# Attention scores of a four-layer kernel on one Trainium2 core: half-height score matmuls, two banks to a tile, and another order of a group's work

## The chip, the core and the metric

The program runs on one of the eight cores of a Trainium2 chip. A core has a matrix engine (TensorE, PE in the profile; its weight loads are listed as PEld), a vector engine (VectorE, DVE), an activation engine (ScalarE, ACT), a general engine (GpSimd, POOL) and a queue that starts transfers (SyncE, SP). Each engine works through its own list of instructions in order and waits on semaphores that the others count up. TensorE writes into PSUM, eight banks of 512 float32 values for each of the 128 partitions; VectorE and ScalarE read them from there. The metric is the device time of the whole program in microseconds (us); lower is better.

## What is computed

Four layers, each an attention followed or accompanied by a gated feed-forward network, on 4 sequences of 256 tokens, 512 wide. The attention has 32 heads of 16 dimensions. In three layers (0, 2 and 3) four query heads share a key head, queries and keys are rotated, and a causal mask applies; layer 1 has its own keys for each head and neither rotation nor mask. Of each attention this is what matters here:

```python
scores = jnp.einsum('bhsd,bhtd->bhst', q, k) / jnp.sqrt(jnp.float32(HEAD_DIM))
scores = jnp.where(causal[None, None], scores, jnp.finfo(scores.dtype).min)   # layers 0, 2, 3
attn = jax.nn.softmax(scores, axis=-1)
out = jnp.einsum('bhst,bhtd->bhsd', attn, v)
```

The four feed-forward networks differ (octonion ternary weights, int4 weights, fp8 scales, low rank); the change does not touch them apart from the names of PSUM banks.

## The kernel before

**Units and groups.** An attention is cut into 8 units `u` (a sequence and one half of the heads: 16 heads), and a unit into 4 groups `g` of 4 heads; `gi = 4u + g` counts the 32 groups of a layer. A unit's queries and keys are first laid out as stacks: a head's 16 dimensions as a rounded value, a low part and the rounded value again, 48 rows, one more row for the maximum, padded to 64. Two heads fill 128 rows. `stack_high` (ACT) and `stack_low` (POOL) write the stacks, `turn_stacks` (PE, L665) turns them with transposes, `take_stacks` (ACT, L1026) and `take_key_stacks` (DVE, L1378) copy them out of PSUM as `qT` and `kT`. Before the change a key's stack stands twice, once above 64 rows of zeros and once below them, so that a matmul of all 128 rows gives the scores of one head alone.

**Scores, twice.** `scores_rows` (L685) makes the scores with queries as partitions, with a second matmul (L691, an identity against a bf16 mask) that adds the mask; `row_max` (DVE, L1370) takes the negated maximum. The maxima of a unit are turned (`turn_max`, L701), copied and placed by a transfer as one row of `qT`. `scores_cols` (L719) then makes the scores with keys as partitions, the maximum already subtracted; `exponentials` (ACT, L1038) writes `probs`; in the causal layers `cut_future` (POOL, L1572) zeroes what lies ahead. `weigh_values` (L739) multiplies the probabilities of the group before by the values, in four column tiles of 32; `take_pv` (ACT, L1045) copies the result, `turn_context` (L750) turns it two groups later, and `context` (DVE, L1394 and L1397) divides by the sum. For every two units the rows are turned (`turn_rows`, L760) and projected (`project_out`, L780); the inputs of later units are projected by `project` (L647). `scores_rows` runs five groups ahead (`LEAD`) of `scores_cols`.

**What sets the order.** The order is written out by hand, for each engine apart, in the function `attention` of that engine: a loop over the 32 groups. Nothing reorders it. In group `g` TensorE has: `project` in g = 0 and 3, `turn_max` in g = 3, first half of `scores_cols`, stacks of tau 0 (g = 0 and 2), first half of `scores_rows`, `weigh_values` of the group before, second half of `scores_cols`, stacks of tau 1, second half of `scores_rows`, `turn_context`, and in every second unit `turn_rows` (g = 2) and `project_out` (g = 3). (In g = 1 the first half of `scores_rows` stands behind `weigh_values`.)

**Banks.** A tile of PSUM is claimed by a key; `Banks` counts the uses of each bank and TensorE waits until the bank's earlier holder has been emptied. A tile of scores is one bank: two heads. `scores_rows` takes turns in banks 0 and 1, `scores_cols` in 2 and 3, everything else in 4 to 7:

```python
def misc_bank():
    misc[0] += 1
    return 4 + misc[0] % 4
```

## Time and profile before

| | us |
|---|---|
| median of 3 runs | 1435.74 (1433.23 to 1436.2) |
| profiled execution, span from first to last instruction | 1432.5 |
| TensorE matmuls busy | 1328.4 (93%) |
| TensorE weight loads busy | 998.8 (70%) |
| VectorE busy | 884.6 (62%) |
| ScalarE busy | 670.5 (47%) |
| GpSimd busy | 389.4 (27%) |

The profile is of one execution, and every duration below is of that one. Its span of 1432.5 us is 3.2 us under the median of the runs; the profile gives no other time of it. A matmul's length includes the time in which it runs through the array while the next has begun, so the distance from start to start is what one costs in a row of many. Where the timeline merges instructions, x is their count and the length runs from the first start to the last end.

### The profile page before, as it was taken

How to read it: one execution, taken by the hardware profiler on the slowest of the kernel's cores; microseconds unless marked ns; L12 is line 12 of the kernel's file. 1: busy time of each engine (PE TensorE's matmuls, PEld its weight loads, DVE VectorE, ACT ScalarE, POOL GpSimd, SP SyncE). 2: the span in 40 equal slices, each digit the busy share in tenths (PEclk: the TensorE clock that was granted, in tenths of full speed). 3: DMA queues.
4: the chain of work that ended last, by engine and by line, in shares of the span. 5: the costliest groups of instructions: out<-in, count | busy, mean ns of one | idle time of the engine just before them, and what ended most of it. 6: DMA issues, size and time to landing. Idle time of an engine off the chain costs nothing.

```text
span 1432.5 us, 22066 instructions
## 1 busy us (share of the span) xinstructions
PE 1328.4 (93%) x8364; PEld 998.8 (70%) x8364; DVE 884.6 (62%) x1661; ACT 670.5 (47%) x1420; POOL 389.4 (27%) x470
## 2 busy tenths in 40 slices
PE   4999899997798999998899999989999879899997
PEld 3888777775465666665688888877777557677775
DVE  7733577777506655567455566467777645777873
ACT  3433365655133654556223333236565447365653
POOL 1000333323011100000433443323343346333331
PEclk9999999999799999999899999999999889999998
DMA  6000000002000000002222232100000300000001
GB/s 261 1 1 0 1 3 2 2 2 97 30 0 1 2 1 2 2 2 92 95 89 88 92 107 89 45 1 2 2 3 2 128 30 1 1 2 2 3 1 60
DMA packets 11610, 48.18 MB, mean 34 GB/s; under 512 B 2793, under 2 KB 3694, under 8 KB 10226
## 3 DMA queue, kind: packets, MB, share of 16 engines
q1 hardware_dynamic: 11506, 46.76, 9.3%
q8 instruction: 69, 1.13, 0.3%
q14 instruction: 35, 0.29, 0.1%
HBM read 44.13 MB, written 2.10 MB: 32 GB/s over the span
## 4 chain that ended last, share of the span: by engine, by line
PE 84%; DVE 10%; ACT 3%; issue 2%; DMA 1%; POOL 0%; SPq 0%; DVEq 0%; ACTq 0%
PE bank L487 18%; PE bank L647 13%; PE bank L518 9%; PE bank L719 7%; PE bank L780 7%; PE bank L685 7%; PE bank L739 7%; PE bank L665 6%; PE bank L691 3%; DVE negmaxs L1370 2%; PE bank L750 2%; DVE negmaxw L1370 2%; PE bank L588 1%; DVE stats L1127 1%; PE bank L760 1%
## 5 line engine op out<-in xcount | busy, mean ns | idle before, releaser
L1572 POOL TENSOR_SCALAR_AFFINE_SELECT probss<-probss 128x512 f32<-128x512 f32 x192 | 134.2, 700 | 334.0 <-ACT probss L1038 334.0
L1370 DVE TENSOR_REDUCE negmaxs<-bank 128x2 f32<-128x512 f32 (+1 forms) x384 | 193.7, 551 | 36.8 <-PE bank L691 35.0
L1038 ACT ACTIVATE probss<-bank 128x256 f32<-128x256 f32 (+1 forms) x384 | 167.9, 492 | 41.9 <-PE bank L719 41.4
L685 PE MATMUL bank<-kTs,qTs 128*128 128x512 f32 (+1 forms) x384 | 135.3, 411 | 5.2 <-DVE kTs L1378 2.8
L1518 POOL TENSOR_TENSOR W_lo<-W_lo_whole,W_hi 128x1536 fp32r<-128x1536 f32 x28 | 98.1, 3504 | 138.4 <-ACT W_hi L889 138.4
L719 PE MATMUL bank<-qTs,kTs 128*128 128x256 f32 (+1 forms) x384 | 117.3, 383 | 4.6 <-ACT probss L1038 3.9
L691 PE MATMUL bank<-mask,identb 128*128 128x256 bf16 x384 | 105.0, 283 | 0.0
L889 ACT ACTIVATE W_hi<-W_lo_whole 128x1536 fp32r<-128x1536 f32 x28 | 41.7, 1488 | 134.7 <-DVE W_lo_whole L1253 134.7
L1378 DVE CAST kTs<-bank 128x512 fp32r<-128x512 f32 x96 | 65.6, 689 | 50.9 <-PE bank L665 50.9
L1274 DVE TENSOR_TENSOR h_lo<-h_lo_whole,h_hi 128x512 fp32r<-128x512 f32 x50 | 73.3, 1465 | 34.9 <-ACT h_hi L911 34.9
L1378 DVE CAST kTw<-bank 128x512 fp32r<-128x512 f32 x64 | 40.9, 685 | 82.3 <-PE bank L665 82.3
L1370 DVE TENSOR_REDUCE negmaxw<-bank 128x2 f32<-128x512 f32 x128 | 81.6, 685 | 14.0 <-PE bank L685 13.6
L487 PE MATMUL bank<-xT_hi,W_hi 128*128 128x512 f32 x224 | 89.2, 398 | 0.0
L487 PE MATMUL bank<-xT_lo,W_hi 128*128 128x512 f32 x224 | 88.6, 396 | 0.0
L685 PEld LDWEIGHTS bank<-kTs,qTs 128*128 128x128 f32 x384 | 74.5, 194 | 20.0 <-DVE negmaxs L1370 11.5
L487 PE MATMUL bank<-xT_hi,W_lo 128*128 128x512 f32 x224 | 88.4, 395 | 0.0
L647 PE MATMUL bank<-Wqkv,xT_whole 128*128 128x512 f32 (+1 forms) x256 | 87.0, 495 | 0.8 <-ACT gate L922 0.8
L987 ACT ACTIVATE qks<-bank 128x320 f32<-128x320 f32 x48 | 21.1, 439 | 141.7 <-PE bank L647 141.6
L739 PE MATMUL bank<-probss,Vs 128*32 128x256 f32 (+1 forms) x1536 | 82.7, 333 | 4.0 <-issue 3.5
L911 ACT ACTIVATE h_hi<-h_lo_whole 128x512 fp32r<-128x512 f32 x72 | 45.4, 630 | 72.3 <-DVE h_lo_whole L1265 46.4
L1038 ACT ACTIVATE probsw<-bank 128x512 f32<-128x512 f32 x128 | 69.6, 599 | 16.6 <-PE bank L719 14.2
L719 PEld LDWEIGHTS bank<-qTs,kTs 128*128 128x128 f32 x384 | 60.4, 191 | 23.4 <-issue 12.7
(219 smaller groups left out, 3162.2 us busy)
## 6 DMA issues: line engine op xcount, KB each, us to landing
W_lo_whole<-in_w SPq DMA_DIRECT2D x28, 768.0 KB, 4.2
Wqkv_whole<-in_Wqkv SPq DMA_DIRECT2D x3, 1536.0 KB, 10.6
Wo_lo_whole<-in_Wo SPq DMA_DIRECT2D x4, 1024.0 KB, 6.2
Wqkv<-in_Wqkv SPq DMA_DIRECT2D x1, 3072.0 KB, 10.6
Wdown_whole<-in_Wd SPq DMA_DIRECT2D x1, 2816.0 KB, 15.2
x<-in_x SPq DMA_DIRECT2D x4, 512.0 KB, 5.9
out<-x SPq DMA_DIRECT2D x8, 256.0 KB, 2.2
V_lo_whole<-in_V SPq DMA_DIRECT2D x1, 1408.0 KB
```

Source lines behind the costliest of these rows:

```text
L487: ins = mm(ps[:], lh, rh, start=(c == 0), stop=(c == len(terms) - 1))
L518: ins = mm(B.tensor(key)[:], lh, rh, start=(j == 0 and c == 0), stop=(j == C - 1 and c == len(terms) - 1))
L647: ins = mm(ps[:, 0:width], lh, rh, start=(c == 0), stop=(c == len(terms) - 1))
L685: ins = mm(ps[:, 0:2 * nk].rearrange("p (h k) -> p h k", h=2), A[l].qT[u % 2][:, 2 * g + pl, qb * P:(qb + 1) * P], A[l].kT[u % 2][:, slot: ...
L691: ins = mm(dst, identb[:], mask[:].rearrange("p (h k) -> p h k", h=2), start=False, stop=True)
L719: ins = mm(ps[:, pairs[0] * nq:pairs[1] * nq].rearrange("p (h q) -> p h q", h=n), A[l].kT[u % 2][:, key_slot(l, g, 2 * g + pairs[0], par), ...
L739: ins = mm(ps[32 * i:32 * i + 32, q0:SEQ], A[l].Vflat[u % 4][:, (kb * A[l].vh + kv) * CELL:(kb * A[l].vh + kv) * CELL + 32], A[l].probs[gi ...
L780: ins = mm(ps[:], lh, rh, start=(c == 0), stop=(c == len(terms) - 1))
L1038: nc.scalar.activation(A[l].probs[gi % 2][:, kb, par:4:2, q0:SEQ], B.tensor(key)[:, 0:2 * nq].rearrange("p (h q) -> p h q", h=2), ACT.Exp, ...
L1370: v.tensor_reduce(A[l].negmax[u % 2][:, qb, 2 * g + pl:2 * g + pl + 9:8], B.tensor(key)[:, 0:2 * nk].rearrange("p (h k) -> p h k", h=2), A ...
L1378: v.tensor_copy(A[l].kT[u % 2][:, 4 * w:4 * w + 4, tau * P:(tau + 1) * P], B.tensor(key)[:].rearrange("p (a t) -> p a t", a=4)).then_inc(B ...
L1572: gp.affine_select(out=blk, in_=blk, compare_op=ALU.is_ge, fill=0.0, base=0, pattern=[[0, 4], [1, P]], channel_multiplier=-1).then_inc(cau ...
```

## The change

**Matmuls of 64 rows.** The zero rows in the key stacks go. A head of a pair is multiplied in the upper 64 rows of the array (`par` 0) and the other in the lower 64 (`par` 1), each into a bank of its own; the mask is added in the same way by four bf16 matmuls of 64 rows with 128 columns (`cut_rows`, `cut_keys`). `kT` has half the slots, and fewer key transposes fill it. Weights are permuted on the host for this.

**Tiles of two banks.** A tile of scores now is all four heads of a group: two adjacent banks, one `row_max` and one `exponentials` instruction in place of two.

**Order and banks.** The loop of TensorE is written anew; ScalarE's and VectorE's loops follow it. Core of the diff:

```diff
-    def claim(self, key, bank):
-        self.where[key] = (bank, self.uses[bank])
+    def claim(self, key, bank, n=1):
+
+        earlier = [self.emptied(k) for k in dict.fromkeys(self.holder[bank:bank + n]) if k is not None]
+        self.where[key] = (bank, self.uses[bank], n)
         self.uses[bank] += 1
+        self.holder[bank:bank + n] = [key] * n
+        return self.tensor(key), earlier
...
-            def misc_bank():
-                misc[0] += 1
-                return 4 + misc[0] % 4
+            def next_bank(n=1):
+
+                if n == 2:
+                    ring[0] += ring[0] % 2
+                bank = ring[0] % 8
+                ring[0] += n
+                return bank
...
+                key = ("S", l, u, g, qb)
+                ps = claim(key, bank, 2)
                 for pl in range(2):
+                    for par in range(2):
+                        r = slice(64 * par, 64 * par + 64)
+                        ins = mm(ps[:, par, pl * nk:(pl + 1) * nk], A[l].qT[u % 2][r, 2 * g + pl, qb * P:(qb + 1) * P],
+                                 A[l].kT[u % 2][r, key_slot(l, g, pl), 0:nk], start=(pl == 0),
+                                 stop=(pl == 1 and not CAUSAL[l]))
+                if CAUSAL[l]:
+                    for j in range(2):
+                        for par in range(2):
+                            r = slice(64 * par, 64 * par + 64)
+                            k0 = nk - P + 64 * j
+                            dst = ps[:, par, 0:2 * nk].rearrange("p (h k) -> p h k", h=2)[:, :, k0:k0 + 64]
+                            ins = mm(dst, cut_rows[r, j, :], cut_keys[r, j, :, :], start=False, stop=(j == 1))
+                ins.then_inc(B.fills(key), 1)
...
                 for gi in range(GROUPS * UNITS):
                     u, g = divmod(gi, GROUPS)
 
                     ahead = gi + LEAD < GROUPS * UNITS
+                    if g == 0 and u + 1 < UNITS:
+                        turn_stacks(l, u + 1, 1)
+                    if g == 2 and u + 2 < UNITS:
+                        turn_stacks(l, u + 2, 0)
                     if g == 0 and u + 2 < UNITS:
                         project(l, u + 2, 1)
+                    if g == 3 and u + 1 < UNITS:
+                        turn_max(l, u + 1)
                     if g == 3 and u + 3 < UNITS:
                         project(l, u + 3, 0)
-                    if g == 3 and u + 1 < UNITS:
-                        turn_max(l, u + 1)
-                    scores_cols(l, u, g, 0)
-                    if g == 0 and u + 1 < UNITS:
-
-                        turn_stacks(l, u + 1, 0, 1)
-                    if g == 2 and u + 2 < UNITS:
-
-                        turn_stacks(l, u + 2, 0, 0)
-                    if ahead and g != 1:
-                        scores_rows(l, gi + LEAD, 0)
-                    if gi >= 1:
-                        weigh_values(l, gi - 1)
-                    if ahead and g == 1:
-
-                        scores_rows(l, gi + LEAD, 0)
-                    scores_cols(l, u, g, 1)
...
+
+                    for part in range(2):
+                        if ahead:
+                            scores_rows(l, gi + LEAD, part, 4 * part)
+                        scores_cols(l, u, g, part, 4 * part + 2)
+                        ring[0] = 4 - 4 * part
+                        if part == 0 and gi >= 1:
+                            weigh_values(l, gi - 1)
                     if gi >= 2:
                         turn_context(l, gi - 2)
...
+                key = ("S", l, u, g, qb)
+                dve.wait_ge(*B.filled(key))
+                v.tensor_reduce(A[l].negmax[u % 2][:, qb, :].rearrange("p (b h) -> p b h", b=2)[:, :, 2 * g:2 * g + 2],
+                                B.tensor(key)[:, :, 0:2 * nk].rearrange("p b (h k) -> p b h k", h=2),
+                                AX.X, ALU.max, negate=True).then_inc(B.empties(key), 1)
```

`turn_stacks` now takes both tau in one go and `take_stacks` and `take_key_stacks` follow it. ScalarE's loop has, for each group: `take_stacks`, `take_projection`, first half of `exponentials`, `take_pv`, second half of `exponentials`, `stack_high`, `take_rows`. Here `ring[0]` is what sets the banks: after the first part it is 4, so `weigh_values` takes bank 4; after the second it is 0, so `turn_context` takes bank 0, and what follows it takes 1, 2, 3 and so on.

**TensorE's list, a plain group** (g = 1 of the second unit, first causal layer), from the values matmuls on. A name such as `bank4_emptied` is the semaphore that counts the copies out of that bank (of a two-bank tile, out of its first bank); the numbers in a tile's name tell buffers apart. Before:

```order
L739 MATMUL bank<-probss_103,Vs_82 32x256 [waits bank2_emptied,bank3_emptied,causal_cut,bank6_emptied]
L739 MATMUL bank<-probss_103,Vs_82 32x256 x3
L739 MATMUL bank<-probss_103,Vs_82 32x128 x4
L685 MATMUL bank<-kTs_98,qTs_97 128x256 [waits bank4_emptied,bank7_emptied,bank1_emptied,bank5_emptied]
L691 MATMUL bank<-mask,identb 128x256
L685 MATMUL bank<-kTs_98,qTs_97 128x256 [waits bank0_emptied]
L691 MATMUL bank<-mask,identb 128x256
L719 MATMUL bank<-qTs_99,kTs_100 128x256 [waits bank3_emptied]
L719 MATMUL bank<-qTs_99,kTs_100 128x256 [waits bank2_emptied]
L685 MATMUL bank<-kTs_98,qTs_97 128x512 [waits bank1_emptied]
L691 MATMUL bank<-mask,identb 128x2x128
L685 MATMUL bank<-kTs_98,qTs_97 128x512 [waits bank0_emptied]
```

Of the change, from the last two matmuls of the first half on:

```order
L718 MATMUL bank<-qTs_99,kTs_100 128x512 [waits bank2_emptied]
L718 MATMUL bank<-qTs_99,kTs_100 128x512
L737 MATMUL bank<-probss_103,Vs_82 32x256 [waits bank2_emptied,bank3_emptied,causal_cut,bank4_emptied]
L737 MATMUL bank<-probss_103,Vs_82 32x256 x3
L737 MATMUL bank<-probss_103,Vs_82 32x128 x4
L686 MATMUL bank<-kTs_98,qTs_97 128x256 [waits bank4_emptied]
L686 MATMUL bank<-kTs_98,qTs_97 128x256 x3
L695 MATMUL bank<-cut_keys,cut_rows 128x2x64 x4
L718 MATMUL bank<-qTs_99,kTs_100 128x256 [waits bank6_emptied]
L718 MATMUL bank<-qTs_99,kTs_100 128x256
L747 MATMUL bank<-ident,pvs_106 128x128 [waits bank4_emptied,bank0_emptied]
L747 MATMUL bank<-ident,pvs_106 128x128
```

The first half of `scores_rows` has moved ahead of this place; the second half stands directly behind the values matmuls and waits for bank 4, the bank which these have just filled.

**TensorE's list at g = 2**, where the stacks of a later unit are turned. Before:

```order
L719 MATMUL bank<-qTs_99,kTs_100 128x512 [waits bank3_emptied]
L719 MATMUL bank<-qTs_99,kTs_100 128x512 [waits bank2_emptied]
L665 MATMUL bank<-ident_r,qstacks_87 128x128 [waits stack_lo,bank4_emptied,stack_hi,pads_set]
L665 MATMUL bank<-ident_r,qstacks_87 128x128 x3
L665 MATMUL bank<-ident_r,kstacks_89 128x128 [waits bank5_emptied]
L665 MATMUL bank<-ident_r,kstacks_89 128x128 x3
L685 MATMUL bank<-kTs_98,qTs_97 128x256 [waits bank1_emptied]
L691 MATMUL bank<-mask,identb 128x256
L685 MATMUL bank<-kTs_98,qTs_97 128x256 [waits bank0_emptied]
L691 MATMUL bank<-mask,identb 128x256
L739 MATMUL bank<-probss_104,Vs_82 32x256 [waits bank2_emptied,bank3_emptied,causal_cut,bank6_emptied]
```

Of the change:

```order
L655 MATMUL bank<-ident_r,qstacks_87 128x128 [waits stack_lo,bank0_emptied,stack_hi,pads_set]
L655 MATMUL bank<-ident_r,qstacks_87 128x128 x3
L655 MATMUL bank<-ident_r,qstacks_88 128x128 [waits stack_lo,bank2_emptied,stack_hi,pads_set]
L655 MATMUL bank<-ident_r,qstacks_88 128x128 x3
L667 MATMUL bank<-ident_r,kstacks_89 128x128 [waits bank2_emptied]
L667 MATMUL bank<-ident_r,kstacks_90 128x128
L686 MATMUL bank<-kTs_98,qTs_97 128x128 [waits bank1_emptied,bank0_emptied]
L686 MATMUL bank<-kTs_98,qTs_97 128x128 x3
L695 MATMUL bank<-cut_keys,cut_rows 128x2x64 x4
L718 MATMUL bank<-qTs_99,kTs_100 128x512 [waits bank3_emptied,bank2_emptied]
L718 MATMUL bank<-qTs_99,kTs_100 128x512
```

Both tau of the stacks stand ahead of the group's scores now, with the waits for `stack_hi` and `stack_lo` of both; before, the second tau stood behind the first half.

**VectorE's list of the same plain group.** Before:

```order
L1370 TENSOR_REDUCE negmaxs_111<-bank 128x2 [waits bank1_filled]
L1370 TENSOR_REDUCE negmaxs_111<-bank 128x2 [waits bank0_filled]
L1370 TENSOR_REDUCE negmaxs_111<-bank 128x2 [waits bank1_filled]
L1370 TENSOR_REDUCE negmaxs_111<-bank 128x2 [waits bank0_filled]
L1394 RECIPROCAL recips_116<-bank 128x8 [waits bank6_emptied,bank7_filled]
L1397 TENSOR_TENSOR ctxs_107<-bank,recips_116 128x2x64 [waits reciprocal_ready]
```

Of the change:

```order
L1343 TENSOR_REDUCE negmaxs_111<-bank 128x2x2 [waits bank0_filled]
L1343 TENSOR_REDUCE negmaxs_111<-bank 128x2x2 [waits bank4_filled]
L1371 RECIPROCAL recips_116<-bank 128x8 [waits bank0_emptied,bank0_filled]
L1374 TENSOR_TENSOR ctxs_107<-bank,recips_116 128x2x64 [waits reciprocal_ready]
L1353 CAST kTs_100<-bank 128x256 [waits bank3_filled]
```

Two reductions take the place of four; the division (L1371, L1374) reads bank 0, as the first of the reductions does, and stands behind the second.

## Rows read from the trace of the kernel before

**Rows 1.** The page, part 1: busy us of each engine, share of the span, instructions.

```profile
PE 1328.4 (93%) x8364; PEld 998.8 (70%) x8364; DVE 884.6 (62%) x1661; ACT 670.5 (47%) x1420; POOL 389.4 (27%) x470
```

**Rows 2.** Busy time by stretch, two stretches: length, engines with counts, PEclk (granted clock), DMA.

```profile
165.28:172.10 6.82, 4.30 (x21) 4.30 (x22) 4.41 (x9) 2.43 (x7) 1.41 (x3) 0.50 0.00 1
...
210.00:259.00 49.00, 48.92 (x415) 37.90 (x414) 37.52 (x86) 29.83 (x78) 17.86 (x28) 1.00 0.01 2
```

**Rows 3.** Timeline of PE, first causal layer, values matmuls: start us, length us, engine, line.

```profile
211.32 0.86 PE L739 MATMUL bank<-probss,Vs 128*32 128x256 f32 x16
...
231.29 0.86 PE L739 MATMUL bank<-probss,Vs 128*32 128x256 f32 x16
...
235.91 0.86 PE L739 MATMUL bank<-probss,Vs 128*32 128x256 f32 x16
...
242.92 0.86 PE L739 MATMUL bank<-probss,Vs 128*32 128x256 f32 x16
...
254.43 0.86 PE L739 MATMUL bank<-probss,Vs 128*32 128x256 f32 x16
...
257.76 0.86 PE L739 MATMUL bank<-probss,Vs 128*32 128x256 f32 x16
```

**Rows 4.** Timeline of all engines in one group (u=2, g=3).

```profile
241.79 0.71 PE L719 MATMUL bank<-qTs,kTs 128*128 128x512 f32 x2
...
242.36 1.08 ACT L1038 ACTIVATE probss<-bank 128x512 f32<-128x512 f32 x2
...
243.45 0.48 DVE L1354 TENSOR_TENSOR rope_coss<-qks,cos 128x320 f32<-128x320 f32 x1
...
243.84 0.38 ACT L1045 ACTIVATE pvs<-bank 128x256 f32<-128x256 f32 x1 [0.40 <-PE bank L739]
...
245.29 1.28 DVE L1370 TENSOR_REDUCE negmaxs<-bank 128x2 f32<-128x512 f32 x2
...
246.72 0.29 DVE L1397 TENSOR_TENSOR ctxs<-bank,recips 128x128 f32<-128x128 f32 x1
```

**Rows 5.** Timeline, the first of a group's score tiles and its first maximum.

```profile
183.19 0.19 PEld L685 LDWEIGHTS bank<-kTs,qTs 128*128 128x128 f32 x1 [0.46 <-DVE negmaxs L1370]
...
183.86 1.29 DVE L1370 TENSOR_REDUCE negmaxs<-bank 128x2 f32<-128x512 f32 x2 [0.39 <-PE bank L691]
```

**Rows 6.** Timeline, copies that build the stacks, and one that takes them from PSUM.

```profile
233.60 0.64 ACT L1015 ACTIVATE qstacks<-rope_coss 128x512 fp32r<-128x512 f32 x1
...
234.71 0.74 POOL L1556 TENSOR_TENSOR qstacks<-rope_coss,qstacks 128x256 fp32r<-128x256 f32 x1 [0.30 <-ACT kstacks L1021]
...
235.62 0.60 ACT L1026 ACTIVATE qTs<-bank 128x512 fp32r<-128x512 f32 x1
```

**Rows 7.** Timeline of PE: projections, four key transposes, two score tiles of 256 columns.

```profile
244.90 0.47 PE L780 MATMUL bank<-Wo_hi,ctxTs 128*128 128x512 f32 x1
...
250.59 0.34 PE L647 MATMUL bank<-Wqkv_hi,xT_hi 128*128 128x384 f32 x1
...
252.70 0.62 PE L719 MATMUL bank<-qTs,kTs 128*128 128x512 f32 x2
...
253.45 0.50 PE L665 MATMUL bank<-ident_r,kstacks 128*128 128x128 f32 x4
...
253.79 0.35 PE L685 MATMUL bank<-kTs,qTs 128*128 128x256 f32 x1
...
254.02 0.36 PE L685 MATMUL bank<-kTs,qTs 128*128 128x256 f32 x1
```

**Rows 8.** Timeline, the layer without mask: values matmuls, a weight load, a projection.

```profile
517.17 0.59 PEld L739 LDWEIGHTS bank<-probsw,Vw 128*32 128x32 f32 x16 [0.37 <-issue]
...
521.04 1.07 PE L739 MATMUL bank<-probsw,Vw 128*32 128x256 f32 x16
...
530.74 5.33 PE L647 MATMUL bank<-Wqkv,xT_whole 128*128 128x512 f32 x16
...
557.38 1.07 PE L739 MATMUL bank<-probsw,Vw 128*32 128x256 f32 x16
```

370 lines of the change are left out of this document (166 added, 204 removed).

## The prediction

> **What bounds the kernel now.** I read the page's busy times first: TensorE is busy for 1328.4 of 1432.5 us, VectorE 884.6, ScalarE 670.5 [rows 1]. Then a stretch inside an attention: of 49.0 us TensorE is busy for 48.92, at full granted clock, VectorE for 37.52 and ScalarE for 29.83 [rows 2]. So TensorE's work is the time there, and VectorE would be next at 77%. The rhythm comes from the starts of the values matmuls, one per group [rows 3]: 4.62 us from g = 1 to 2, 7.01 to g = 3, 11.51 to g = 0, 3.33 to g = 1, together 26.47 for a unit that also projects its output and 19.97 (211.32 to 231.29) for one that doesn't: 46.4 a pair. Without a mask the longer unit takes 36.3 (521.04 to 557.38) [rows 8].
>
> **What the change takes away.** If the two halves of the array work side by side, a causal group loses half its score time. A tile of 256 columns with its mask costs 0.23 us from start to start (253.79, 254.02 [rows 7]), one of 512 another 0.11 for 256 columns at 2.4 GHz; each group has two of each, and columns scores of two times 512 and two times 256: (1.14 + 0.64)/2 = 0.9 us. Twelve of a unit's 32 stack transposes go, at 0.085 us (253.45 to 253.79, four) [rows 7]: 0.26 a group. Over 96 causal groups and 32 others that is about 150 us of TensorE's list. VectorE and ScalarE also save a fixed 0.1 us or so wherever two instructions become one. All this counts only where TensorE's list is the bound.
>
> **What it adds: one ring of waits through three engines.** The order shows it. In a group TensorE makes rows part 0 (banks 0, 1), columns part 0 (2, 3), values (bank 4); rows part 1 claims banks 4 and 5 and so waits for `take_pv`. ScalarE has `take_pv` behind the first `exponentials`. Then `turn_context` takes bank 0, and the next group's first instruction claims bank 0, so it waits for VectorE's division, which stands behind the maximum of part 1. Before, values and context had four banks in turn, and nothing of the kind waited.
>
> Step by step, c being the start of columns part 0, X that of rows part 1. The low end has both halves side by side, the high end one after the other.
> - c to X. The first exponential began 0.57 after the first column matmul (241.79, 242.36); two took 1.08, one of double size about 1.0; `take_pv` 0.38 [rows 4]; 0.1 for the semaphore: 2.05. In sequence, another 512 columns, 0.22: 2.27. The values matmuls (0.86, rows 3) end inside this, but nothing follows them.
> - X to the next c. First tile of 512 columns to its maximum: 0.67 [rows 5]. Four heads' maximum: 1.2 in place of 1.28 for two. The division ends 0.44 after the maximum (246.57, 247.01) [rows 4]. Semaphore 0.1, rows part 0 0.24 [rows 7]: 2.65. In sequence, 0.3 and 0.25 more: 3.2.
>
> A plain causal group thus takes 4.7 to 5.5 us however little TensorE has to do. The four intervals of a causal unit:
> - g = 0 to 1: the rotation (243.45 to 245.29, 1.84 [rows 4]) stands between the two maxima. c - 0.24 + 0.5 + 0.65 + 1.84 = c + 2.75, about when part 1 is filled (c + 2.72). 4.8 to 5.5, against 3.33.
> - g = 1 to 2: both tau of the stacks now precede the group. Part 1 is filled and exponentiated at X + 0.8 + 0.54; `stack_high` takes 1.11 less 0.25 for one copy fewer (233.60 to 234.71), `stack_low` 0.74 [rows 6] and, by half the elements, about 0.4: X + 3.4. Four transposes and their copy, 0.5 + 0.60 [rows 6], empty bank 2 at X + 4.65, semaphores counted. 2.05 + 4.65 = 6.7 to 7.2, against 4.62.
> - g = 2 to 3: `turn_max` now precedes the projection and waits for the last maximum, X + 1.97. Then 0.14, the projection 2.11 (250.59 to 252.70) [rows 7], 0.3 until the array is empty (an estimate from the 0.37 of [rows 8]), 0.24: X + 4.8. 6.9 to 7.5, against 7.01. Little is lost, since the projection fills what was a hole.
> - g = 3 to 0: X = c + 2.05; part 1, columns and context to X + 0.95; output projection 5.69 (244.90 to 250.59) [rows 7]; stacks 0.85; projection 2.11; 0.3 + 0.24: 12.2 to 12.6, against 11.51. Without the output projection the next one waits for bank 4, that is for the maximum at c + 4.08: 6.8 to 7.3.
>
> Sums: 30.6 to 32.8 against 26.47, and 25.2 to 27.5 against 19.97; a mean excess of 4.6 to 6.9 a unit. Seven units have it (the last makes no rows): 32 to 48. The prologue copies fewer key tiles: -1.5. Three layers: 92 to 140.
>
> The layer without mask: 4.6 to 5.2 for a plain group by the same two steps with 1024 elements on both. At g = 2 exponentials (1.0), `stack_high` (1.3) and `stack_low` (1.5) give 8.3. At g = 3 the values wait for the copy of the key stack in bank 4: 10.7. At g = 0, projection 5.1 (5.33 less the last one's running out [rows 8]; eight matmuls of 512 columns and eight of 256, so 0.42 for 512), output projection (16 by 0.42) 6.7, stacks 1.4 and waits: 17.4. Sum 41 against 36.3; seven units: 30 to 42.
>
> The rest (feed-forward, loads) has the same work and cover; banks are renamed. In the last unit of layers 0 to 2 the next layer's transposes share the ring: 0 to 3 us each, left to the range. Total: +122 to +182. I take +150, the middle, because no row has two matmuls in different halves, so both ends are open: 1432.5 + 150 = 1582.5 in the profile. The median of the runs lies 3.2 above the span: 1586.
>
> **Two rules weighed.** A change of tile shape empties the array here: the weight load of the values matmuls came 0.37 us after the last one [rows 8]. The Trainium skill (TensorEngine Tiling, Key Properties) says that a change of tiling mode drains the TensorE; by that rule, the trace agrees, 64-row tiles bring two more drains a group. Of these most fall into the ring's waits, so the sum stays. The Trainium skill (TensorEngine Tiling, Key Properties) also says that different tiles can load and multiply in parallel; no row here shows it, and by it the sum would be the low end, about 1558.
>
> **Rivals.**
> - TensorE's list stays the bound and the ring hides. The 150 us go, two drains a group at 0.27 come back (128 x 0.54 = 69): about 1355. For it: 48.92 of 49.0 us busy. Against it: the waits stand in the order, and a ring of 4.7 us cannot run in 3.33 or 4.6. It would decide if ScalarE's and VectorE's double-size instructions took clearly less than two single ones; each ring has 2.2 us of such work, and would have to lose 1.1 of it. 6%.
> - The granted clock falls with the emptier array. Before, it stood at 0.50 over 6.82 us in which TensorE was busy for 4.30, behind a long wait [rows 2]. After, waits are of 0.9 to 1.5 us, shorter than that one. If a fifth of the attention ran at half clock, its projections and stacks (some 20 us a pair) would double there: 16 pairs x 4 = 64 more, 1650. 10%.
> - The halves work in turn throughout: the high end, 1618. This is inside the forecast's own range, not apart.
> - The ring binds but its largest terms overlap (stack copies earlier than I count, rotation before the maximum's data): half the excess, 1510. 8%.
>
> **How the numbers follow.** The ring as worked out: 76%, 1586, its own range 1555 to 1625. Clock 10% at 1650, half the excess 8% at 1510, TensorE-bound 6% at 1355. The range 1520 to 1650 leaves out the last, part of the clock case and the far end of the third. A measurement of this kernel can tell about 0.2% from no change, some 3 us. Faster: only the first rival, 0.06; same 0.02; slower 0.92.
>
> **What would show it.** In the profile after: TensorE's busy share down to some 70%; before the rows scores of part 1 (L686) idle time of near 1 us put down to ScalarE's copy of the values (L1026), once a group; before those of part 0, or the projection, idle time put down to VectorE (L1374 or L1343); a plain group of 4.7 to 5.5 us and g = 1 to 2 of 6.7 to 7.2; the maximum of 1024 elements about 1.2 us, the exponential 1.0. Side by side halves show as starts a few ns apart. The prediction is wrong if values matmuls of plain groups start under 4 us apart, or if the waits before L686 are short.

## The result, and the profile after

The changed kernel took **1671.5 us** (median of 4 runs, 1665.4 to 1673.8) against 1436.0 (1433.2 to 1440.7): a ratio of 1.164, 95% interval 1.160 to 1.167. The forecast was 1586, its range 1520 to 1650. The direction was right, and so was the ring of waits; what the forecast left out is TensorE's clock. Of +235 us it had +150.

The page of the changed kernel: busy us of the engines (compare [rows 1]) and the granted TensorE clock in 40 slices of the span (tenths of full speed).

```profile
PE 1391.4 (83%) x8844; PEld 1014.6 (61%) x8844; DVE 810.3 (48%) x1309; ACT 656.1 (39%) x1100; POOL 368.5 (22%) x462
...
PEclk9999677767796978777999999877876789778858
```

The first surprise stands in the first row. TensorE is busy for 63 us *longer* than before, although an attention now holds less work for it. The PEclk row says why: in the slices of the attentions, which lie among 5 to 19 and 26 to 40, it shows mostly 5 to 8.

Busy time by stretch, from the first to the last values matmul of each layer (length, busy us of PE, PEld, DVE, ACT, POOL with counts, granted clock, DMA share, GB/s). Changed kernel:

```profile
187.10:418.60 231.50, 184.23 (x1461) 130.31 (x1461) 107.81 (x214) 94.75 (x174) 53.99 (x89) 0.71 0.04 16
525.40:798.20 272.80, 217.46 (x1466) 131.99 (x1467) 110.30 (x168) 114.92 (x172) 19.25 (x27) 0.81 0.04 13
1089.50:1314.10 224.60, 177.41 (x1460) 126.74 (x1460) 108.00 (x215) 92.42 (x170) 53.74 (x89) 0.75 0.06 22
1437.80:1653.50 215.70, 172.12 (x1436) 122.42 (x1436) 97.91 (x189) 89.77 (x165) 51.52 (x86) 0.75 0.03 9
sum 944.60, PE 751.22 PEld 511.46 DVE 424.02 ACT 391.87 POOL 178.50; mean PE 187.81 PEld 127.87 DVE 106.00 ACT 97.97 POOL 44.62
```

The same four stretches of the kernel before, the first of them and the sum:

```profile
191.50:353.70 162.20, 156.35 (x1336) 117.66 (x1335) 121.34 (x280) 98.19 (x250) 59.60 (x89) 1.00 0.07 23
...
sum 691.20, PE 671.50 PEld 488.75 DVE 482.87 ACT 404.26 POOL 193.76; mean PE 167.87 PEld 122.19 DVE 120.72 ACT 101.06 POOL 48.44
```

All of the loss is in the attentions: 944.6 against 691.2 us, +253. What lies between and around them is 15 us shorter than before (726.6 of 1671.2 us against 741.3 of 1432.5). A granted clock of 0.71 is a mixture of the two levels, 0.50 (1.2 GHz) and 1.00 (2.4 GHz): 2 x (1 - 0.71) = 58% of 231.5 us at the half. By the same sum over the four rows **458 of 944.6 us ran at the half clock**; before, in the same stretches, 3. (The shares are printed to 0.01, so such a sum is good to some 7 us.)

One causal unit of layer 3 (u = 3), timeline of PE in the changed kernel: the five values matmuls (L737) that bound its four intervals, and the matmuls that wait.

```profile
1525.20 0.86 PE L737 MATMUL bank<-probss,Vs 128*32 128x256 f32 x16
...
1526.72 0.50 PE L686 MATMUL bank<-kTs,qTs 64*128 64x256 f32 x4 [0.67 <-ACT pvs L1026]
...
1527.46 0.44 PE L747 MATMUL bank<-ident,pvs 128*128 128x128 f32 x2
...
1529.32 0.44 PE L686 MATMUL bank<-kTs,qTs 64*128 64x128 f32 x4 [1.42 <-DVE ctxs L1374]
...
1530.10 0.86 PE L737 MATMUL bank<-probss,Vs 128*32 128x256 f32 x16
...
1535.17 0.72 PE L655 MATMUL bank<-ident_r,qstacks 128*128 128x128 f32 x4 [2.08 <-POOL kstacks L1530]
...
1537.48 1.51 PE L737 MATMUL bank<-probss,Vs 128*32 128x256 f32 x16
...
1546.64 0.86 PE L737 MATMUL bank<-probss,Vs 128*32 128x256 f32 x16
...
1553.23 0.86 PE L737 MATMUL bank<-probss,Vs 128*32 128x256 f32 x16
```

Here stand the waits that the forecast had read from the order: rows part 1 behind ScalarE's copy of the values (0.67), the next rows part 0 behind VectorE's division (1.42), the stacks of tau 1 behind GpSimd (2.08). The intervals are 4.90, 7.38, 9.16, 6.59 us, in sum 28.03; before they were 3.33, 4.62, 6.13 and 5.91. And the same sixteen values matmuls take 0.86 us in four places and 1.51 at 1537.48: that group ran at the half clock, and so did the first half of the projection behind it. Over the four intervals the granted clock was 1.00, 0.78, 0.62 and 1.00.

What TensorE waited for in all (total us, times, longest). Of the rows left out between, one (29.0 us, L457) lies almost wholly outside the attentions; those further down are smaller:

```profile
PE bank L686 <- ACT pvs L1026: 45.1, 78, 0.7
PE bank L655 <- POOL kstacks L1530: 32.3, 18, 2.1
...
PE bank L686 <- DVE ctxs L1374: 26.9, 21, 1.4
PE bank L655 <- POOL kstackw L1530: 18.5, 6, 3.2
PE bank L686 <- ACT pvw L1026: 13.7, 26, 1.1
PE bank L718 <- DVE xT_lo L1127: 12.5, 6, 2.5
```

The double-size instructions came as forecast, 1.0 and 1.2 us (timeline, changed kernel: four heads in one exponential and in one maximum):

```profile
1504.42 1.02 ACT L1019 ACTIVATE probss<-bank 128x1024 f32<-128x1024 f32 x1 [1.12 <-PE bank L718]
...
1507.34 1.22 DVE L1343 TENSOR_REDUCE negmaxs<-bank 128x4 f32<-128x1024 f32 x1 [2.83 <-PE bank L695]
```

And the halves of the array work side by side. This is the timeline of PE for a window of 0.015 us: both matmuls of a pair have begun by its end. Together they take 0.39 us; one of this size took 0.35 before (253.79 [rows 7]), and a second one behind it would end 0.11 later.

```profile
213.29 0.39 PE L686 MATMUL bank<-kTs,qTs 64*128 64x256 f32 x2 [0.67 <-ACT pvs L1026]
```

### The profile page after: what moved, and what is told of

It reads as the page before. It is cut to its first block, busy times and chain, and to the rows that moved or that the text cites. A ratio compares the mean times of both kernels' runs of the same rounds, so it can differ in the third digit from the quotient of the medians.

```text
span 1671.2 us, 22690 instructions
## 1 busy us (share of the span) xinstructions
PE 1391.4 (83%) x8844; PEld 1014.6 (61%) x8844; DVE 810.3 (48%) x1309; ACT 656.1 (39%) x1100; POOL 368.5 (22%) x462
## 4 chain that ended last, share of the span: by engine, by line
PE 70%; DVE 12%; ACT 8%; issue 7%; POOL 2%; DMA 0%; DVEq 0%; ACTq 0%; SPq 0%
PE bank L490 15%; PE bank L642 12%; PE bank L520 8%; PE bank L686 7%; PE bank L775 6%; PE bank L737 6%; PE bank L718 4%; DVE negmaxs L1343 2%; PE bank L655 2%; PE bank L695 2%; PE bank L747 2%; ACT probss L1019 2%; PE bank L756 1%; PE bank L667 1%; ACT pvs L1026 1%
## 5 line engine op out<-in xcount | busy, mean ns | idle before, releaser
L1343 DVE TENSOR_REDUCE negmaxs<-bank 128x4 f32<-128x512 f32 x192 | 181.7, 957 | 252.8 <-PE bank L695 252.6
L1019 ACT ACTIVATE probss<-bank 128x1024 f32<-128x1024 f32 x192 | 155.3, 811 | 215.9 <-PE bank L718 215.5
L686 PE MATMUL bank<-kTs,qTs 64*128 64x128 f32 (+1 forms) x768 | 114.6, 386 | 83.6 <-ACT pvs L1026 45.1
L686 PEld LDWEIGHTS bank<-kTs,qTs 64*128 64x128 f32 x768 | 78.3, 246 | 133.7 <-ACT pvs L1026 73.2
L1343 DVE TENSOR_REDUCE negmaxw<-bank 128x4 f32<-128x1024 f32 x64 | 77.4, 1222 | 112.6 <-PE bank L686 112.6
L718 PE MATMUL bank<-qTs,kTs 64*128 64x256 f32 (+1 forms) x384 | 102.7, 527 | 18.1 <-DVE xT_lo L1127 8.6
L737 PE MATMUL bank<-probss,Vs 128*32 128x256 f32 (+1 forms) x1536 | 110.6, 420 | 7.7 <-issue 4.9
L1008 ACT ACTIVATE qTs<-bank 128x512 fp32r<-128x512 f32 x96 | 54.3, 597 | 95.9 <-PE bank L655 95.9
L1019 ACT ACTIVATE probsw<-bank 128x1024 f32<-128x1024 f32 x64 | 65.3, 1023 | 67.1 <-PE bank L718 66.8
L655 PE MATMUL bank<-ident_r,qstacks 128*128 128x128 f32 x384 | 56.5, 298 | 39.3 <-POOL kstacks L1530 32.3
L737 PEld LDWEIGHTS bank<-probss,Vs 128*32 128x32 f32 x1536 | 48.6, 131 | 66.2 <-issue 49.8
L642 PE MATMUL bank<-Wqkv_hi,xT_hi 128*128 128x384 f32 x192 | 77.2, 402 | 0.0
```

What stands on the lines that cost most here:

```text
L642: ins = mm(ps[:, 0:width], lh, rh, start=(c == 0), stop=(c == len(terms) - 1))
L655: ins = nc.tensor.transpose(ps[:, p * P:(p + 1) * P].bitcast(F32R), A[l].qstack[tau][:, 8 * half + 2 * p:8 * half + 2 * p + 2, :] .rearran ...
L686: ins = mm(ps[:, par, pl * nk:(pl + 1) * nk], A[l].qT[u % 2][r, 2 * g + pl, qb * P:(qb + 1) * P], A[l].kT[u % 2][r, key_slot(l, g, pl), 0: ...
L718: ins = mm(ps[:, par, pairs[0] * nq:pairs[1] * nq].rearrange("p (h q) -> p h q", h=n), A[l].kT[u % 2][r, key_slot(l, g, pairs[0]), kb * P: ...
L737: ins = mm(ps[32 * i:32 * i + 32, q0:SEQ], A[l].Vflat[u % 4][:, (kb * A[l].vh + kv) * CELL:(kb * A[l].vh + kv) * CELL + 32], A[l].probs[gi ...
L1019: nc.scalar.activation(A[l].probs[gi % 2][:, kb, :, q0:SEQ].rearrange("p (b h) q -> p b h q", b=2), B.tensor(key)[:, :, 0:2 * nq].rearrang ...
```

## The experiments

The theories were: A, the ring of waits at its low end, and the half clock on top; B, the waits alone are longer than forecast and the clock is only their sign; C, the 64-row matmuls cost more than they save; D, the new order costs, not the banks. Here is what all the runs gave. "Half" is the time at half clock in the four attentions, worked out as above; the intervals are those of the unit shown above (u = 3, layer 3), from values matmul to values matmul.

| kernel | us, median | ratio to before (95%) | attentions, us | half, us | intervals g0-1, 1-2, 2-3, 3-0 |
|---|---|---|---|---|---|
| before | 1436 | 1 | 691 | 3 | 3.33, 4.62, 6.13, 5.91 |
| changed | 1671.5 | 1.164 (1.160 to 1.167) | 945 | 458 | 4.90, 7.38, 9.16, 6.59 |
| fill | 1606.0 | 1.117 (1.115 to 1.120) | 882 | 51 | 4.93, 6.84, 7.22, 6.57 |
| stacks | 1598.3 | 1.113 (1.108 to 1.119) | 871 | 355 | 4.89, 5.92, 9.62, 6.55 |
| fill_stacks | 1551.1 | 1.081 (1.079 to 1.082) | 823 | 12 | 4.96, 4.74, 7.65, 6.60 |
| ctx | 1632.1 | 1.137 (1.134 to 1.140) | 906 | 289 | 3.84, 9.35, 8.10, 6.62 |
| oldorder | 1478.7 | 1.029 (1.027 to 1.031) | 733 | 133 | 2.79, 4.59, 6.06, 6.02 |
| oldorder_fill | 1458.5 | 1.016 (1.013 to 1.018) | 714 | 7 | 3.00, 4.59, 6.68, 6.20 |
| banks | 1552.8 | 1.082 (1.079 to 1.084) | 799 | 200 | 4.32, 6.31, 7.01, 6.96 |
| banks_stacks | 1459.4 | 1.017 (1.015 to 1.019) | 711 | 61 | 4.30, 3.52, 6.39, 6.96 |
| banks_stacks_proj | 1466.0 | 1.023 (1.021 to 1.024) | 716 | 73 | 4.30, 3.52, 6.47, 6.96 |
| banks_stacks_fill | 1458.3 | 1.016 (1.014 to 1.019) | 704 | 10 | 4.31, 3.52, 6.60, 6.95 |
| rope_last | 1470.7 | 1.025 (1.024 to 1.026) | 725 | 83 | 3.61, 4.97, 6.38, 6.26 |
| rope_cols | 1494.1 | 1.040 (1.039 to 1.042) | 741 | 132 | 3.61, 5.33, 7.89, 6.48 |

### fill: give TensorE something to do in the waits

```diff
+            def fill(bank, n):
+                if B.holder[bank] is not None:
+                    pe.wait_ge(*B.emptied(B.holder[bank]))
+                for _ in range(n):
+                    mm(B.ps[:, bank, 0:256], cut_rows[:, 0, :], cut_keys[:].rearrange("p a b c -> p (a b c)"), ...)
...
                             weigh_values(l, gi - 1)
+                        if part == 0:
+                            fill(7, 6)
                     if gi >= 2:
                         turn_context(l, gi - 2)
+                    if g < 3:
+                        fill(3, (10, 12, 10)[g])
```

> Edit: the changed kernel with extra bf16 matmuls of 256 columns whose results are overwritten or never read: 6 after the values matmuls, and 10, 12 and 10 at the end of groups 0, 1 and 2, in the waits. Nothing of the work is left out. Theory A (the ring costs about +150 as forecast, the other +85 are TensorE at half granted clock): the granted clock rises from 0.83 to over 0.93 and the time falls in spite of more work, to about 1600 (1570 to 1630). Theory B (the surplus is longer waits and drains in the ring, the clock changes nothing that the ring does not hide): the time stays at 1671 or rises by up to 40, whatever the clock does.

Measured: 1606.0 us, 65.5 less than the changed kernel **with 1792 matmuls more**. The first and the last attention and the sum:

```profile
187.70:398.20 210.50, 193.19 (x1898) 142.69 (x1897) 108.20 (x214) 94.23 (x175) 53.48 (x89) 0.97 0.05 18
...
1392.10:1591.40 199.30, 186.05 (x1870) 138.43 (x1869) 97.35 (x189) 89.20 (x165) 51.31 (x86) 0.99 0.03 10
sum 881.50, PE 811.15 PEld 579.06 DVE 423.86 ACT 389.03 POOL 177.58; mean PE 202.79 PEld 144.77 DVE 105.97 ACT 97.26 POOL 44.40
```

The same unit in this kernel (PE timeline):

```profile
1471.55 0.86 PE L745 MATMUL bank<-probss,Vs 128*32 128x256 f32 x16
...
1476.48 0.86 PE L745 MATMUL bank<-probss,Vs 128*32 128x256 f32 x16
...
1483.32 0.86 PE L745 MATMUL bank<-probss,Vs 128*32 128x256 f32 x16
...
1490.54 0.86 PE L745 MATMUL bank<-probss,Vs 128*32 128x256 f32 x16
...
1497.11 0.86 PE L745 MATMUL bank<-probss,Vs 128*32 128x256 f32 x16
```

At full clock the four intervals are 4.93, 6.84, 7.22, 6.57. The forecast had 4.8 to 5.5, 6.7 to 7.2, 6.9 to 7.5 and 6.8 to 7.3: the ring as worked out, at its low end, the last a little under it. What waits for what in the ring is the same here. The extra matmuls wait for the bank that they write, but in all of the run that came to 1.0 us (its 1792 matmuls, L455). What changed is that TensorE's own work between the waits ran faster: g = 2 to 3 took 7.22 in place of 9.16, and g = 0 to 1, which in the changed kernel is at full clock too, 4.93 and 4.90. So theory B falls, and the clock has a price of its own.

The extra matmuls cost something where there is no wait to hide them. The last unit of layer 3 makes no rows; from its first values matmul to its last it took this in the changed kernel:

```profile
1642.76 0.86 PE L737 MATMUL bank<-probss,Vs 128*32 128x256 f32 x16
...
1653.54 1.38 PE L737 MATMUL bank<-probss,Vs 128*32 128x256 f32 x16 [1.13 <-issue]
```

and this in fill:

```profile
1576.50 0.86 PE L745 MATMUL bank<-probss,Vs 128*32 128x256 f32 x16
...
1591.41 0.86 PE L745 MATMUL bank<-probss,Vs 128*32 128x256 f32 x16 [1.13 <-issue]
```

10.8 against 14.9 us, so 4.1 here; the last units of layers 0 to 2 grew by 4.9, 2.5 and 2.4, in all 14 us. That leaves about 1606 - 14 - 1436 = 156 us for the ring, and 65 (measured) to 79 (with those 14) for the clock. The parting is an estimate: what the extra matmuls cost in other units isn't known, and 51 us of fill are still at the half clock.

### stacks and fill_stacks: the wait for the key stacks, and the clock again

```diff
-                    if g == 2 and u + 2 < UNITS:
+                    if g == 3 and u + 2 < UNITS:
                         turn_stacks(l, u + 2, 0)
```

and likewise for `take_stacks` and `take_key_stacks`; fill_stacks is this together with fill.

> Edit: the changed kernel with the stacks of unit u+2 turned at the start of group 3 in place of group 2, on all three engines. Theory A: the 1.7 us wait for stack_low before the second tau goes and the copies hide behind turn_max and the projection; the interval g = 1 to 2 falls from about 8 to about 5.5, g = 2 to 3 grows by 0.5: 28 units with less 1.5 to 2 us each, 1620 (1600 to 1640). Theory C: no change beyond 1%.

> The changed kernel with its shared turn of banks, with both the extra matmuls in its waits (they keep TensorE's granted clock up and compute nothing that is used) and the stacks of u + 2 turned at g = 3. Against the version with the stacks alone (1598.3, 356 us of attention at half clock) it prices the clock by itself; against the one with the extra matmuls alone (1606.0) it prices the stack's wait at full clock. Theory of the ring and the clock as two costs that add: g=1 to 2 about 5.0 (6.83), g=2 to 3 at 7.5 to 8, unit sum of an odd unit 24 and an even one 30: 1606 less 1.6 to 1.9 us for 19 units, with the extra matmuls no longer hidden beside the stack's wait for some of it: about 1565 to 1575, clock 0.95 or more. Theory of the waits alone (the clock is a sign of the waits and costs nothing by itself): 1598, no change from the version with the stacks.

Measured: 1598.3 and 1551.1. The unit u = 3 of layer 3 in stacks, and then in fill_stacks (columns as above):

```profile
1453.20:1480.18 26.98, 22.42 (x200) 16.46 (x198) 13.74 (x28) 12.53 (x24) 7.09 (x12) 0.75 0.01 2
```

```profile
1413.65:1437.60 23.95, 23.59 (x256) 17.99 (x254) 13.70 (x28) 12.29 (x24) 7.09 (x12) 1.00 0.01 2
```

Moving the stacks one group later saves 73 us without the extra matmuls and 55 with them. The forecast had this wait inside its 6.7 for g = 1 to 2, rightly: with the stacks gone that interval is a plain one, 4.74. The extra matmuls save 47 us here, where 23 to 33 had been expected (1565 to 1575), and bring 355 us at half clock down to 12. The clock costs 65 us at least in the one pair and 47 in the other.

### ctx: the division out of the ring

```diff
-                    if gi >= 2:
-                        turn_context(l, gi - 2)
+                        if part == 0 and gi >= 2:
+                            turn_context(l, gi - 2, 6)
```

and on VectorE `context` between the two maxima, `rope` behind both.

> Edit: the changed kernel with turn_context moved up behind the values matmuls, in bank 6, and VectorE's division before its second maximum, the rotation behind it. Theory A (the ring from rows part 1 through VectorE's division to the next group's rows part 0): a plain group falls from 4.9 to about 3.5 us, no idle time before rows part 0 put down to the division; 1540 (1500 to 1590). Theory C (no ring, the 64-row matmuls and their drains are what costs): the groups keep their length, 1650 to 1680.

Measured: 1632.1, so far less than expected. The first interval became 3.84 as forecast; the second became 9.35. The trace shows a fault of the experiment, in g = 1 (PE timeline of ctx):

```profile
1493.08 0.39 PE L718 MATMUL bank<-qTs,kTs 64*128 64x256 f32 x2 [1.33 <-DVE ctxs L1374]
...
1496.22 0.72 PE L655 MATMUL bank<-ident_r,qstacks 128*128 128x128 f32 x4 [2.29 <-POOL kstacks L1530]
```

Columns part 1 use banks 6 and 7, and I had put the context in 6: the division left one ring and entered another, behind a maximum that itself began late, at 1491.90, after the rotation of the group before. The later exponential then delayed the stacks. The first interval says that the division and the rotation ahead of it set it, but not which of the two, since the edit moved both; of the rest the run says nothing.

### oldorder and oldorder_fill: the 64-row matmuls without the new order

Matmuls, two-bank tiles and single instructions as in the changed kernel, but the loops of before, rows in banks 0 and 1, columns in 2 and 3, all else in 4 to 7:

```diff
-                bank = ring[0] % 8
+                bank = 4 + ring[0] % 4
...
+                    scores_cols(l, u, g, 0, 2)
+                    if g == 0 and u + 1 < UNITS:
+                        turn_stacks(l, u + 1, 1)
+                    if ahead and g != 1:
+                        scores_rows(l, gi + LEAD, 0, 0)
+                    if gi >= 1:
+                        weigh_values(l, gi - 1)
+                    if ahead and g == 1:
+                        scores_rows(l, gi + LEAD, 0, 0)
+                    scores_cols(l, u, g, 1, 2)
+                    if g == 2 and u + 2 < UNITS:
+                        turn_stacks(l, u + 2, 0)
+                    if ahead:
+                        scores_rows(l, gi + LEAD, 1, 0)
```

oldorder_fill adds 4 matmuls as in fill ahead of the last `scores_rows` in g = 0 to 2, and 2 behind it in g = 1 to 3.

> Edit: 64-row matmuls and two-bank tiles of the change, but the order of the kernel before, rows scores always in banks 0 and 1, columns scores in 2 and 3, all else in turn in 4 to 7. Theory A (order and banks make the loss, the matmuls themselves a gain): faster than before, 1390 (1350 to 1430), clock over 0.93. Theory C (the 64-row matmuls and drains cost): slower than before, 1500 to 1650.

> The 64-row matmuls in the order of before, with 4 extra bf16 matmuls of 256 columns ahead of rows part 1 in g = 0 to 2 and 2 behind it in g = 1 to 3 (TensorE waits there for VectorE; they compute nothing that is used). Without them this order took 1478.7, with 133 us of its attention at the half clock, and its units at full clock took 19.5 where the kernel before takes 20.0. Theory that the clock is what this order loses against the kernel before: half the half-clock time comes back at least in part, clock 0.95 or more, 1478.7 less 30 to 45, and the extra matmuls cost up to 10: 1445 (1435 to 1455). Theory that the half clock is only a sign of waits for VectorE: the extra matmuls delay rows part 1, 1480 or more.

Measured: 1478.7, then 1458.5. So 193 of the 235 us lie in the order and its banks together; which of the two it is, the next runs tell. Neither range on record for oldorder held: it is slower than before, but by 43 us and not by 64 or more, and far above the 1390 of theory A. oldorder_fill came out some 13 above its 1445. The unit u = 3 of layer 3 in oldorder:

```profile
1363.79:1383.25 19.46, 17.84 (x203) 13.13 (x199) 13.96 (x28) 12.32 (x25) 7.24 (x13) 1.00 0.01 3
```

19.46 us at full clock against 19.99 before. TensorE's busy time fell from 19.95 to 17.84, and the time hardly followed, since TensorE now waits for the other engines: one maximum of 1.22 us holds both row banks, and in the second and third group of this unit TensorE waits 0.62 and 0.52 us for it (1368.72 and 1370.67).

That isn't because the 64-row matmuls cost what they save. A plain group of the kernel before (PE timeline, from the rows scores of part 0 to the end of the columns scores of the next group's part 0):

```profile
1326.25 0.39 PE L685 MATMUL bank<-kTs,qTs 128*128 128x256 f32 x1
...
1328.10 0.38 PE L750 MATMUL bank<-ident,pvs 128*128 128x128 f32 x2
1328.24 0.71 PE L719 MATMUL bank<-qTs,kTs 128*128 128x512 f32 x2
...
1328.79 0.47 PE L665 MATMUL bank<-ident_r,qstacks 128*128 128x128 f32 x4
```

Start to start, its four blocks of scores take 1.85 + 0.55 = 2.40 us of TensorE's list. In the changed kernel at full clock the same four take 0.74 (1526.72 to 1527.46, in the section on the result) + 0.78 (1529.32 to 1530.10) = 1.52, the changes of tile shape among them counted. The 0.88 us saved a group are what the forecast had (0.9); what it also said holds, that they count only where TensorE's list is the bound. The even units lose in the projection's group (g = 2 to 3 of u = 2: 9.86 against 7.02, at a granted clock of 0.65). The extra matmuls take that back (7.56 there) and cost 1.0 in the odd unit (20.47), in sum -20. So theory C falls. How much of the remaining 23 us of oldorder_fill is the extra matmuls' own cost, and how much that of the tiles of two banks, stays open.

### banks, banks_stacks and banks_stacks_proj: which edge of the ring

Order of the changed kernel; rows always in banks 0 and 1, columns in 2 and 3, all else in turn in 4 to 7:

```diff
-                bank = ring[0] % 8
+                bank = 4 + ring[0] % 4
...
-                            scores_rows(l, gi + LEAD, part, 4 * part)
-                        scores_cols(l, u, g, part, 4 * part + 2)
-                        ring[0] = 4 - 4 * part
+                            scores_rows(l, gi + LEAD, part, 0)
+                        scores_cols(l, u, g, part, 2)
```

banks_stacks adds the edit of stacks; banks_stacks_proj puts `turn_max` behind the projection in g = 3, too.

> Edit: the changed kernel, its order untouched, with other banks: both parts' rows scores in 0 and 1, both parts' columns scores in 2 and 3, all else in turn in 4 to 7. So rows part 1 waits for the first maximum and no longer for take_pv, and the next group's rows part 0 for the second maximum and no longer for the division. Theory A (the ring is made by the shared banks): a plain group falls from 4.9 to 3.3 us at most, g = 1 to 2 stays over 5.5 (stacks), clock over 0.88; 1500 (1470 to 1540). Theory D (the order of the parts makes the loss, not the banks): over 1600.

> Edit: as banks, and the stacks of unit u+2 turned at the start of group 3 in place of group 2. Theory A: the two terms add, 1.5 to 2 us less for each of 28 units: 1450 (1420 to 1480), g = 1 to 2 under 4.6. Theory D: as the kernel stacks, about 1600.

> Edit: as banks_stacks, and the projection of g = 3 ahead of turn_max, as in the kernel before. Theory A: turn_max's wait for the last maximum hides behind the projection, 0.5 to 1 us less for each of some 20 units that project there: 1435 (1405 to 1465). If the maximum is ready anyway: no change from banks_stacks.

Measured: 1552.8, 1459.4 and 1466.0. These two edits take 212 of the 235 us back with the order of the parts left as it is. So it is not the order of scores and values that costs (theory D, which had over 1600 for both), but which banks scores, values and context share, and that both tau of the stacks stand ahead of a group too early. Of the clock nothing was touched: it came back by itself, from 458 us at the half to 61. The last edit gained nothing, where 1435 had been the forecast. `turn_max` waits for only 4.3 us in all in banks_stacks, 0.37 in the unit shown, and the profile puts none of it down to the maximum: there was next to nothing to hide.

What is left of the waits in banks_stacks (PE timeline, same unit):

```profile
1351.94 0.44 PE L686 MATMUL bank<-kTs,qTs 64*128 64x128 f32 x4 [1.52 <-DVE negmaxs L1342]
...
1355.46 0.44 PE L686 MATMUL bank<-kTs,qTs 64*128 64x128 f32 x4 [0.74 <-DVE negmaxs L1342]
...
1366.51 0.44 PE L642 MATMUL bank<-Wqkv_hi,xT_hi 128*128 128x384 f32 x1 [1.06 <-DVE ctxs L1373]
```

Rows part 0 wait for the second maximum, 1.52 us where the rotation stands ahead of it and 0.74 where not. And the projection waits 1.06 us for the division, which empties the bank that it takes: that is the 6.96 of g = 3 to 0 against 5.91 before.

### banks_stacks_fill, rope_last and rope_cols: can it beat the kernel before?

banks_stacks_fill: 5 such matmuls at the end of g = 0 to 2. rope_last moves the rotation behind the division; rope_cols also swaps rows and columns within a part:

```diff
                         row_max(l, gi + LEAD, 0)
-                    if ROPE[l] and g == 0 and u + 2 < UNITS:
-                        rope(l, u + 2, 1)
...
                     if gi >= 2:
                         context(l, gi - 2)
+                    if ROPE[l] and g == 0 and u + 2 < UNITS:
+                        rope(l, u + 2, 1)
```

> The version with rows in banks 0 and 1, cols in 2 and 3 and the stacks at g = 3 (1459.4, 61 us of its attention at half clock), with 5 extra bf16 matmuls of 256 columns at the end of g = 0 to 2, where rows part 0 then waits 0.75 us for the second maximum (1305.03). They compute nothing that is used. Theory of the ring: plain groups are set by VectorE at 3.5 us, so the extra 0.55 us stand in the wait and cost nothing; the clock brings back at most half of 61 less what fell to waits, some 10 us: 1450. Not below the kernel before (1435), since the projections' groups stay at 6.95 against 5.91. Theory without the clock: no change, 1459, or slower by the extra matmuls.

> The bank and stack version (rows always in banks 0 and 1, cols in 2 and 3, the rest in turn in 4 to 7, stacks of u + 2 turned at g = 3) with one more move: VectorE's rotation of the vectors comes behind the second maximum and the division instead of between the two maxima. Theory of the ring: with one pair of banks for the rows, rows part 0 of the next group waits for the second maximum (1322.68 rows, 1.52 us where the rotation stood ahead of it), so the interval g=0 to 1 falls from 4.31 to about 3.55 and the one from g=3 to the next unit's g=0 from 6.95 to about 6.3 in the three layers with a rotation: 18 units by 0.8 and 15 by 0.6, 23 us in all, 1459 to about 1437, at the time of the kernel before. Theory that what is left against the kernel before is TensorE's own drains between tiles of 64 and 128 rows and the half clock: under 8 us of gain, 1452 or more.

> As the version with the rotation moved, and in each part the cols come before the rows. Theory of the ring: the banks of the cols are freed by the shorter instruction (0.64 us of exponential of part 1 against 1.2 of the second maximum), so what waits for the longer one comes half a microsecond later; where rows part 0 still waits (0.2 to 0.9 us a plain group), that wait falls, 2 to 3 us a unit at most: 1437 to about 1425, under the kernel before. Theory that VectorE itself is full in the plain groups (two maxima, the division, 2.9 of 3.5 us): no change, 1437, since its start is then later by what TensorE waits less.

Measured: 1458.3, 1470.7 and 1494.1, for forecasts of 1450, 1437 and 1425. In banks_stacks_fill the half clock went from 61 us to 10 and the median stayed; g = 2 to 3 grew from 6.39 to 6.60, so some of the gain went to the extra matmuls themselves. In rope_last both forecast intervals fell as expected (3.61 and 6.26), and the one between rose from 3.52 to 4.97. The timeline of all engines in that place:

```profile
1360.22 0.98 POOL L1525 TENSOR_TENSOR qstacks<-rope_coss,qstacks 128x256 fp32r<-128x256 f32 x1
...
1360.53 0.86 DVE L1330 TENSOR_TENSOR rope_sins<-qks,sin 128x160 f32<-128x160 f32 x1
...
1362.19 0.68 DVE L1342 TENSOR_REDUCE negmaxs<-bank 128x4 f32<-128x512 f32 x1
...
1362.93 0.50 PE L686 MATMUL bank<-kTs,qTs 64*128 64x256 f32 x4 [1.38 <-DVE negmaxs L1342]
```

Behind the division the rotation stands ahead of the *next* group's first maximum, and rows part 1 wait 1.38 us for that. With one pair of banks for the rows every maximum is an edge of the ring, and the rotation's two microseconds fall on one of them wherever they stand. Swapping rows and columns made it worse (g = 2 to 3: 7.89, half clock 132 us for 83). One of my two theories had a gain of 12 us and the other no change; neither foresaw a loss of 23, and its cause stays open. No version here beats the kernel before.

## Why the prediction was wrong, step by step

- **"What the change takes away"**: right. TensorE's list lost 0.88 us of scores a group for a forecast 0.9; TensorE was not the bound.
- **"One ring of waits through three engines"**: right. The waits are the ones named, in the places named, and undoing the banks and the stacks gives 212 us back (a part of it by way of the clock).
- **The steps and sums of the ring**: right for each step. At full clock c to X (columns part 0 to rows part 1, 211.37 to 213.29 in layer 0) was 1.92 us for 2.05, and X to the next c, here with the rotation, 2.95, together 4.87 for "4.8 to 5.5". Unit sums at nearly full clock (fill, layer 3): 25.56 for 25.2 to 27.5, and 31.48 for 30.6 to 32.8. The halves of the array run side by side, so the high end never applied.
- **That the ring's total came out at 156 for 150** is in part luck. In fill, by the spans of the profiled executions (1608.2 against 1432.5, 6 us further apart than the medians): seven units of three causal layers +116 (forecast 92 to 140), seven of the layer without mask +46 (30 to 42), the four last units +28, of which 14 are the extra matmuls' (0 to 3 each), and everything outside the attentions -15, which the forecast had at nothing. What was counted too low and what was counted too high cancel for the most part.
- **"The granted clock falls with the emptier array"** is the step that failed. It stood among the rivals, with 10% and a price of 64 us, for "a fifth of the attention"; the argument against it was "waits are of 0.9 to 1.5 us, shorter than that one". It should have been part of the main case: 458 of 945 us at the half clock, nearly half, and a cost of 65 to 79 us. The price per microsecond was high rather than low (64 for a fifth would have been some 155 for a half), probably since much of the time at the half clock was waiting for other engines anyway; the share was what was missed. Ring 156 and clock 79 make the 235.
- **Why the argument against it was wrong.** [Rows 2] had the one stretch at 0.50, and the forecast took the *length* of the wait before it as the cause. The changed kernel shows otherwise (PE timeline, layer 0). In the group from 211.37 on TensorE waited twice, 0.67 us (213.29, above) and then this:

```profile
215.89 0.44 PE L686 MATMUL bank<-kTs,qTs 64*128 64x128 f32 x4 [1.42 <-DVE ctxs L1374]
...
216.66 1.51 PE L737 MATMUL bank<-probss,Vs 128*32 128x256 f32 x16
```

  The granted clock was 1.00 from 211.37 to 216.66 and 0.51 in the next 3.24 us, and the values matmuls took 1.51 us for 0.86. So two waits of the size that the forecast took for harmless were enough. The Trainium skill (TensorE: Matmul & The Clock Gate, A second HAM failure mode: psum-queue depth-cycling) describes the like for bf16 matmuls of 512 columns: a TensorE that idles briefly between groups of matmuls as it cycles through PSUM banks, and whose clock swings between the two levels; the trace agrees (0.71 to 0.81 over whole attentions). The rival should have been worked out for all of the attention and put at better than even.
- **"TensorE's busy share down to some 70%"**: wrong, and only in part for the same reason. It is 83%. Matmuls at the half clock are longer, so a busy share doesn't show idle time when the clock moves. But with the clock nearly whole it doesn't fall to 70% either: in banks_stacks TensorE is busy for 617 us of the attentions and before for 671, 54 less and not the 150 of its list. Probably each new wait counts the last matmul's run through the array as busy.
- **The layer without mask**: forecast +30 to 42 us for seven units; in fill, at a granted clock of 0.95, they take 242.7 against 196.8, +46. Its g = 1 to 2 was forecast as 8.3 and is 8.9 to 9.6 there, g = 2 to 3 as 10.7 and is 11.3 to 12.1: the stack's chain through GpSimd was too short in the sum.
- **The last unit of layers 0 to 2**, "0 to 3 us each": it grew by 4.6 to 5.3 (21.1, 20.2 and 19.6 against 16.4, 14.8 and 15.0), with columns waiting for the next layer's transposes (`xT_lo`, 12.5 us in all above).
- **The rival "TensorE's list stays the bound"** (1355): not even in the old order, where oldorder_fill is 103 us above it.

## What to carry to other kernels

When a change puts regular short waits into TensorE's list, work out two costs: the waits, and TensorE's own work between them at the half clock, over the whole stretch and not over a fifth of it. Extra matmuls in the waits are a quick test that tells the two apart, if they wait for nothing themselves (1.0 us here) and their own cost is taken off where there is no wait to hide them (14 us here). And in a fixed order the banks are edges too: a value that takes a bank ahead of a matmul ties that matmul to whoever empties the value.

## What the runs showed of the hardware

- The clock fell under waits of 0.5 to 2.1 us (seven in the 28 us of the unit shown; in layer 0 behind 0.67 and 1.42 alone), and time at the half clock went from 458 us to 51 when they were filled with unneeded work and to 61 when most of them were removed. Its price was not constant: 65 us for 407 us less at half clock (changed to fill), 47 for 343 (stacks to fill_stacks), 20 for 126 in the old order, 1 for 51 in banks_stacks, each net of the extra matmuls.
- Two 64-row matmuls in the two halves of the array run side by side, 0.39 us for the pair. They take 0.88 us of 2.40 off a group's scores on TensorE's list; of that, 0.5 us of 20 reached an odd unit of oldorder, and nothing the kernel's time.
- VectorE's and GpSimd's instructions slow each other down. The two halves of the sine product are the same work; beside no GpSimd instruction one took this (VectorE timeline, rope_last):

```profile
1349.07 0.32 DVE L1330 TENSOR_TENSOR rope_sins<-qks,sin 128x160 f32<-128x160 f32 x1
```

  against 0.86 at 1360.53 above, where GpSimd's subtraction took 0.98 in place of 0.74 [rows 6]. The Trainium skill (GPSIMD Engine Reference, Specifications) says that GpSimd shares its SBUF interfaces with VectorE and contends with instructions of two SBUF inputs; the trace agrees. It happened in 15 of rope_last's 18 rotations at g = 0 and in none of banks_stacks, where this product took 0.32. So it put more than half a microsecond ahead of the next maximum each time, which is one more reason why rope_last missed.
